# A four-block transformer kernel: the values' projection moves ahead in TensorE's order of the 16-head stages

## The reference

```
x = x + gate_a * attention(norm(x) * (1 + scale_a) + shift_a)
x = x + gate_m * mlp(norm(x) * (1 + scale_m) + shift_m)
```

```
q, k, v = rows of h @ W ;  q, k = rotary(q), rotary(k)
p = softmax(q @ k.T / 4) ;  out = (p @ v) @ W_out + b
```

## Time and profile before

| | |
|---|---|
| median of 3 runs | 2127.19 us (2124.84 to 2128.36) |
| the profiled execution's own time | 2128.56 us |
| its span | 2126.8 us |
| TensorE matmul busy | 1911.8 us, 90% |
| VectorE busy | 1319.5 us, 62% |
| ScalarE busy | 994.4 us, 47% |
| GpSimd busy | 787.6 us, 37% |
| TensorE's mean granted clock | 0.960 of full speed |

### The profile page before, as it was taken

How to read it: one execution, slowest core, us unless ns; L and a number is a source line. 1 busy time by engine, 2 the same in 40 slices (tenths; PEclk the granted TensorE clock), 3 DMA queues, 4 the chain that set the end, 5 groups by cost and what they waited for, 6 DMA issues and landing times. The chain is left out here.

```text
span 2126.8 us, 44677 instructions
## 1 busy us (share of the span) xinstructions
PE 1911.8 (90%) x17318; PEld 1485.0 (70%) x17318; DVE 1319.5 (62%) x2028; ACT 994.4 (47%) x1693; POOL 787.6 (37%) x737
## 2 busy tenths in 40 slices
PE   5999999999979998688988899969999799988898
PEld 4777777777867776466766777747777677766675
DVE  4454555555554555588898577768888555544455
ACT  3433433443336666365666344324555466643222
POOL 1220211121123334566677333456878533340000
PEclk8999999999999999799999999979999899999999
DMA  5100000000010000100000000010000000003222
GB/s 184 70 2 2 2 2 2 2 2 2 2 41 21 0 0 1 45 2 3 2 2 2 27 0 0 0 41 2 2 0 2 27 5 0 0 21 103 75 70 80
DMA packets 26300, 44.73 MB, mean 21 GB/s; under 512 B 4240, under 2 KB 12240, under 8 KB 26000
## 3 DMA queue, kind: packets, MB, share of 16 engines
q1 hardware_dynamic: 24848, 42.01, 6.0%
q10 hardware_dynamic: 1280, 0.23, 0.1%
HBM read 35.94 MB, written 6.29 MB: 20 GB/s over the span
## 5 line engine op out<-in xcount | busy, mean ns | idle before, releaser
L1205 DVE TENSOR_TENSOR Glb<-Gfb,Ghb 128x512 fp32r<-128x512 f32 x176 | 165.2, 948 | 97.6 <-ACT Ghb L1156 95.9
L443 PE MATMUL bank<-HH,W1b 128*128 128x512 f32 x448 | 184.9, 413 | 16.1 <-PEq L1511 7.1
L325 POOL TENSOR_TENSOR Tm<-Dv,MOD 128x512 f32<-128x512 f32 x94 | 108.4, 1173 | 236.9 <-DVE Dv L382 159.1
L444 PE MATMUL bank<-HL,W1b 128*128 128x512 f32 x448 | 177.3, 396 | 0.0
L445 PE MATMUL bank<-HH,W1b 128*128 128x512 f32 x448 | 177.2, 396 | 0.0
L443 PE MATMUL O<-Ghb,W2b 128*128 128x512 f32 x352 | 142.9, 406 | 37.1 <-DVE Glb L1205 37.0
L463 POOL TENSOR_TENSOR spare<-RT 128x1 f32<-128x1 f32 x32 | 6.4, 201 | 401.1 <-DVE RT L454 401.1
L314 POOL TENSOR_TENSOR XS<-Tm 128x512 f32<-128x512 f32 x48 | 69.8, 1454 | 219.1 <-ACT Tm L280 214.2
L445 PE MATMUL O<-Ghb,W2b 128*128 128x512 f32 x352 | 138.0, 392 | 0.0
L444 PE MATMUL O<-Glb,W2b 128*128 128x512 f32 x352 | 137.8, 391 | 0.0
L1386 PE MATMUL bank<-WQKa,HH 128*128 128x512 f32 x256 | 91.6, 441 | 38.8 <-DVE HL L390 16.6
(11 more groups left out here) (262 smaller groups left out, 5161.6 us busy)
## 6 DMA issues: line engine op xcount, KB each, us to landing
w<-l_w_dram SPq DMA_DIRECT2D x33, 256.0 KB, 3.4
X<-xT_dram SPq DMA_DIRECT2D x16, 256.0 KB, 6.7
out_dram<-XO SPq DMA_DIRECT2D x8, 512.0 KB, 2.7
wm<-w_mods_dram SPq DMA_DIRECT2D x4, 768.0 KB, 5.1
W2b_f<-l_w_dram SPq DMA_DIRECT2D x11, 256.0 KB, 5.5
WQK_f<-l_wqk_dram SPq DMA_DIRECT2D x8, 256.0 KB, 8.6
W1b_0f<-l_w_dram SPq DMA_DIRECT2D x8, 256.0 KB, 3.7
wm<-w_mods_dram SPq DMA_DIRECT2D x4, 384.0 KB, 6.3
```

The source lines that it names most:

```text
L325: nc.gpsimd.tensor_tensor(Tm[:, k].rearrange("p (b t) -> p b t", t=T), Dv[:, k].rearrange("p (b t) -> p b t", t=T), m, ALU.mult).then_inc( ...
L443: nc.tensor.matmul(out, w_lo_ap, x_hi, start=first, stop=False)
L444: nc.tensor.matmul(out, w_hi_ap, x_lo, start=False, stop=False)
L1205: nc.vector.tensor_tensor(Gl[m % gb][:], gf, Gh[m % gb][:].bitcast(F32), ALU.subtract).then_inc(g_lo.h, 1)
```

## The change

In TensorE's step the two lines that call `pe_v` move up: from behind `out_t` to right behind `weights_t`. They now stand ahead of the mean, the variance, `qk_t` and `out_t`. The arguments, the waits inside and the programs of the other engines are the same.

```diff
                             if not first:
                                 weights_t(pe, tt - 1, prev, more or not tail)
+                            if ahead(t, more, tail, 2):
+                                pe_v(pe, tt + 2, (t + 2) % TL, c + (t + 2) // TL, (p + (t + 2) // TL) % 2, False)
                             if t == 1 and f.centred:
                                 pe.wait_ge(out_taken.h, out_taken.at(2 * (tt - 2)))
                                 f.pe_mean(pe, cc)
...
                                 qk_t(pe, tt + 1, (t + 1) % TL)
                             if past(tt, 2):
                                 out_t(pe, tt - 2)
-                            if ahead(t, more, tail, 2):
-                                pe_v(pe, tt + 2, (t + 2) % TL, c + (t + 2) // TL, (p + (t + 2) // TL) % 2, False)
                             if not first:
                                 weigh(pe, tt - 1, prev)
```

## The result

The changed kernel took 2140.99 us (median of 4 runs, 2137.16 to 2143.66) beside 2127.65 of the kernel before: a ratio of 1.0064, with a 95% interval of 1.0045 to 1.0083. It is slower by 13 us, as forecast (2143).

What follows compares the result with a forecast made beforehand. PE, busy for 90% of the span, was the engine to look at, with ACT's OS chain hidden by 0.6 us. Second stage +14.3 and first +1.3 made +15.6 on 2127.2: 2143 us (chance 0.55), range 2130 to 2152.

Steps and rivals of the forecast that it cites:

- The switches: Two more changes of array shape on PE around the moved values, 0.17 us each; L1529 then starts 1.19 after the weights' transposes.
- Rival (b): No change: moved loads hide the array-shape changes, so what follows the values starts 0.85 later, not 1.19; 2129 us, chance 0.10.
- Second stage, t = 0 and t = 2: The 0.56 stall goes, but the output projection waits for ACT's OS: +0.1 to +0.15 a step, 13 steps, +2.0 us.
- Rival (a): Faster: the hole is filled and ACT keeps up, saving 0.3 in each of 28 steps; about 2117 us, chance 0.08.
- Second stage, t = 3: Variance already filled the hole; L1529, OS and output projection come later: +0.65 a step, +3.9 us in six chunks.
- Second stage, t = 1: Mean and L1529 start 1.2 later; DVE's KB, HL and next projection have no slack: +1.2 a chunk, +7.2 in six.
- Second stage in all: Sum of the second stage's terms, 2.0 + 3.9 + 7.2 + 1.2 = +14.3 us.
- The last chunk's 1.2: In the second stage's last chunk PE waits for GpSimd, up to 3.8, which follows the norm of t = 3: +1.2 once.
- First stage: Net +0.4 in seven chunks from t = 2 and t = 3, less 1.5 at t = 1: +1.3 us, bounds -4 and +6.
- the 1.5 from the clock: First stage, t = 1: values inside PE's idle time win back at least 0.5 in three lower-clock steps, -1.5 us.
- Rival (c): Slower by half: t = 1 costs its 7.2 + 1.2, the rest is absorbed or given back; 2135 us, chance 0.14.
- Rival (d): Slower still: second-stage t = 1 steps fall to the lower clock, 6 to 12 times 0.8; 2148 to 2153 us, chance 0.13.

Runs made afterwards that it cites:

- the other profile: The changed kernel, but with the values behind the output transposes again at t = 1 of the second stage: 2132.86 us beside 2126.98 for the kernel before.

## Why the prediction was right, point by point

*The switches: 0.17 each.* Right: L1529 stands 1.19 behind the transposes of the weights (1528.14 to 1529.33), and every next start after the values has its 0.17. Rival (b), by which loads are pulled ahead across such a change, is out.

*Second stage, t = 0 and t = 2: +0.1 to +0.15, the hole turned into a wait for OS.* Right, shown by the two kernels with OS first: +0.12 and +0.13 in the table's chunk. Over all 13 steps it made 1.1 instead of 2.0, since these steps did not grow in the last two ordinary chunks. Rival (a) needed the chain to be shorter than PE's remaining work. With OS first it is, and that version gains.

*Second stage, t = 3: +0.65.* The step itself grew by 0.57. The statement behind it, that GpSimd's and DVE's work has room for the later norm in the ordinary chunks, was wrong: t = 3 alone also puts 0.28 on t = 1. The term was 0.85 in all.

*Second stage, t = 1: +1.2.* The mechanism was right (mean, L1529, masked copies, KB, HL, projection), the size was not: 0.63 by itself. The step that failed is "no slack"; HL's duration is not fixed and gave 0.47 back. The two errors cancel in part: forecast 2.15 a chunk from t = 0 to t = 3, measured 34.58 - 32.95 = 1.63.

*Second stage in all: +14.3.* It measured +8.6 from first to last scores. The six t = 1 steps grew by 4.1 in all, not by 7.2: two of them (10.44 and 10.21 us in the changed kernel) by only 0.3, with HL at 1.29 and 1.22 us. The seven t = 3 steps made 3.5 (forecast 3.9), t = 0 and t = 2 made 1.1. The last chunk's 1.2 did not appear: its t = 1 step, where PE waits for GpSimd anyway, got shorter by 0.85 (9.55 instead of 10.40), and its t = 2 longer by 0.60. The 3.8 that the prediction quotes for this wait stands in that t = 2 step; at t = 1 it was 2.70.

*First stage: +1.3.* It measured +5.0 in this pair and would be +1.9 by the other profile with the same code in it. The chain behind t = 3 was right: t = 2 was 7.75 instead of 7.88, t = 3 8.22 instead of 8.09, t = 0 9.82 instead of 9.41. Chunks 1 to 6 (counted from 0) grew by 1.6 in all (1.7 in the other profile), where the forecast says 0.9. The first chunk (+1.3) and the last (+2.1) make up the rest of the 5.0, and in the other profile they did not grow. Of the three t = 1 steps with a lower clock, one went from 10.72 to 10.24, as forecast; another went from 10.74 to 9.91, but a longer t = 3 followed (9.49 instead of 8.40); the third drop came up at t = 0 instead. So the 1.5 from the clock is not confirmed, and what it is worth stays open. Two windows of the changed kernel show a drop at t = 0 and one in the last chunk:

```profile
1026.10:1036.90 10.80, 9.27 (x93) 6.84 (x92) 10.28 (x18) 5.22 (x12) 6.62 (x8) 0.84 0.00 0
1154.80:1163.30 8.50, 7.93 (x74) 6.49 (x74) 6.29 (x11) 6.87 (x14) 7.70 (x8) 0.59 0.01 2
```

Rival (c), by which t = 1 costs all and the rest is absorbed, is out: t = 3 grew and t = 1 by less. Rival (d), the clock in the second stage, did not come.

So the forecast of +15.6 beside the measured +13.3 has the sign and the mechanism from its steps. That the sum is this near is partly luck: in the profiled pair (+15.1) the second stage was set 6 too high, the first 4 too low, and 1.5 lie outside both.

## What to carry to other kernels

When work of PE is moved into a stall, ask what it had been hiding where it stood. Here it covered a chain of four copies on another engine, and the stall came back 3 us further on; shortening that chain (one copy ahead of two) turned the same move into a gain, while by itself it gave nothing. And a move that costs 0.1 us in one step of a pipeline can cost 0.6 or 0.9 in its neighbour: made everywhere it lost 0.6%, made at t = 0 and t = 2 alone nothing that can be told, and there with the shorter chain it gained 0.4%.

## What the runs showed of the hardware

HL, a VectorE operation of 1024 elements a partition, took 1.22 us alone and 1.88 to 2.23 in the ordinary chunks of the kernel before, with GpSimd's full operations beside it. The records show how it came to that, here in the kernel before:

```profile
1500.11 1.29 POOL L1481 TENSOR_TENSOR RAa<-QNa,RCa 128x512 f32<-128x512 f32 x1
1500.41 2.06 DVE L390 TENSOR_TENSOR HL<-H,HH 128x1024 fp32r<-128x1024 f32 x1
1501.34 2.41 POOL L1483 TENSOR_TENSOR RBa<-QNa,RCa 128x256 f32<-128x256 f32 x2
```

GpSimd's L1481 was running when HL began, and ended at 1501.40; HL ended at 1502.48, 1.08 later. Of the six ordinary chunks of this kernel and the six of the one with the values early at t = 1 of the second stage, eleven have a GpSimd operation running at HL's start, and HL ended 1.08 or 1.09 us behind it in every one. In the twelfth none ran, and HL took 1.21.

It goes both ways. In the kernel with GpSimd's work cut down, two tiny operations took 1.39 us together while HL ran (0.22, and 1.23 for the one that began during HL), and 0.37 where they ran just ahead of it:

```profile
1495.50 1.39 POOL L1484 TENSOR_TENSOR RBa<-QNa,RCa 128x8 f32<-128x8 f32 x2
1495.62 1.22 DVE L390 TENSOR_TENSOR HL<-H,HH 128x1024 fp32r<-128x1024 f32 x1
```

```profile
1499.19 0.37 POOL L1484 TENSOR_TENSOR RBa<-QNa,RCa 128x8 f32<-128x8 f32 x2
1500.42 1.22 DVE L390 TENSOR_TENSOR HL<-H,HH 128x1024 fp32r<-128x1024 f32 x1
```

The first pair is of the kernel with the values late, the second of the one with them early at t = 1. In these records the operation that had begun went on and the other came behind it, so the duration of such an operation is not a constant that a sum can take from one row.
